# Moving the residual layernorm of a sandwich block from a stage of its own into the attention loop

## The reference

```
a  = layernorm(x)
s  = a @ W_spin.T + b_spin
g  = mean(s, tokens) @ W_global.T
e  = s @ W_J.T
P  = softmax(e @ s.T / 32)
attn = tanh(beta * (s + g + P @ s))
x1 = x + layernorm(attn)
y  = layernorm(x1)
h  = silu(y @ Wg.T / 127) * (y @ Wu.T / 127)     # int weights, 3072 x 1024
out = x1 + layernorm(h @ Wd.T / 127)
```

## Time and profile before

| | before |
|---|---|
| median of 3 runs | 1401.44 us (1400.98 to 1401.98) |
| profiled execution, its own time | 1401.98 us |
| its span on the slowest core (core 0) | 1399.8 us |
| spans of the 8 cores | 1385.7 to 1399.8 us |
| TensorE matmul busy | 1182.5 us, 84% |
| VectorE, ScalarE, GpSimd busy | 372.0, 208.5, 73.1 us |
| idle time of TensorE ahead of L955 | 115.5 us, behind DMA transposes into `xn2T` |
| DMA | 131.00 MB, mean 94 GB/s |

### The profile page before, as it was taken

How to read it: one execution, slowest core, us unless ns; L and a number is a source line. 1 busy time by engine, 2 the same in 40 slices (tenths; PEclk the granted TensorE clock), 3 DMA queues, 4 the chain that set the end, 5 groups by cost and what they waited for, 6 DMA issues and landing times.

```text
span 1399.8 us, 14416 instructions; the slowest of 8 cores (1385.7 to 1399.8 us)
## 1 busy us (share of the span) xinstructions
PE 1182.5 (84%) x5274; PEld 513.5 (37%) x5274; DVE 372.0 (27%) x608; ACT 208.5 (15%) x331; POOL 73.1 (5%) x92
## 2 busy tenths in 40 slices
PE   0788887869999999999999011499999999999997
PEld 0233332223444444444444000144444444444443
DVE  2243343301121111112111545521111122133443
ACT  0111111211122112212221100111111111100000
POOL 0011110000000000000000100111111111000000
PEclk9999998989999999999999555699999999999999
DMA  9746565661223224322321988573645453023322
GB/s 196 151 112 146 140 146 126 157 116 36 45 59 70 53 45 64 71 48 46 68 61 30 222 209 238 130 79 35 86 45 77 46 67 39 1 91 98 113 91 90
DMA packets 230388, 131.00 MB, mean 94 GB/s; under 512 B 204720, under 2 KB 204720, under 8 KB 230320
## 3 DMA queue, kind: packets, MB, share of 16 engines
q1 hardware_dynamic: 102688, 79.74, 22.2%
q0 software_dynamic: 57744, 29.37, 16.1%
q10 hardware_dynamic: 69888, 20.98, 7.3%
HBM read 92.31 MB, written 25.17 MB: 84 GB/s over the span
## 4 chain that ended last, share of the span: by engine, by line
PE 77%; DMA 12%; DVE 6%; issue 2%; SPq 1%; ACT 1%; ACTq 1%; DVEq 0%
PE ps_q L544 16%; PE ps_pv L651 16%; PE ps_d L1103 12%; PE ps_g L955 12%; PE ps_u L967 11%; DMA xnT_sb<-xn_bf 7%; PE ps_s L257 6%; PE ps_e L306 2%; DMA xn2T<-xn_bf 2%; DMA xs<-x 2%; DVE x_buf L822 1%; PE ps_pv L428 1%; PE ps_s L253 1%; SPq L891 1%; DVE ln_tmp L812 1%
## 5 line engine op out<-in xcount | busy, mean ns | idle before, releaser
L955 PE MATMUL ps_g<-xn2T,wg_sb 128*128 128x512 bf16 x768 | 187.8, 389 | 115.5 <-DMA xn2T<-xn_bf 115.5
L544 PE MATMUL ps_q<-s_FM,ebuf 128*128 128x512 bf16 x1024 | 225.6, 381 | 9.1 <-DMA ebuf<-e_sc 9.1
L651 PE MATMUL ps_pv<-s_tok,PT_sb 128*128 128x512 bf16 x1024 | 225.3, 381 | 0.9 <-DVE g_bc L494 0.9
L967 PE MATMUL ps_u<-xn2T,wu_sb 128*128 128x512 bf16 x768 | 183.8, 383 | 0.0
L1103 PE MATMUL ps_d<-wdT_sb,h_act 128*128 128x512 bf16 x768 | 165.9, 379 | 1.1 <-DVE h_act L990 1.1
L955 PEld LDWEIGHTS ps_g<-xn2T,wg_sb 128*128 128x128 bf16 x768 | 76.1, 100 | 210.9 <-issue 124.0
L544 PEld LDWEIGHTS ps_q<-s_FM,ebuf 128*128 128x128 bf16 x1024 | 100.2, 98 | 131.9 <-issue 12.8
L651 PEld LDWEIGHTS ps_pv<-s_tok,PT_sb 128*128 128x128 bf16 x1024 | 100.6, 98 | 123.1 <-issue 3.5
L257 PE MATMUL ps_s<-wspT_sb,xnT_sb 128*128 128x512 bf16 x512 | 136.8, 415 | 0.0
L990 DVE SCALAR_TENSOR_TENSOR h_act<-silu_b,ps_u 128x512 bf16<-128x512 f32 x96 | 65.8, 687 | 262.0 <-PE ps_u L967 262.0
L967 PEld LDWEIGHTS ps_u<-xn2T,wu_sb 128*128 128x128 bf16 x768 | 75.9, 99 | 93.3 <-issue 4.8
(11 more groups left out here) (67 smaller groups left out, 421.0 us busy)
## 6 DMA issues: line engine op xcount, KB each, us to landing
xs<-x SPq DMA_DIRECT2D x24, 1024.0 KB, 7.2
x_sc<-x_buf SPq DMA_DIRECT2D x16, 512.0 KB, 4.6
xs<-x_sc SPq DMA_DIRECT2D x16, 512.0 KB, 4.2
out<-out_b SPq DMA_DIRECT2D x16, 512.0 KB, 5.0
wg_sb<-wgT POOLq DMA_DIRECT2D x24, 256.0 KB, 4.5
wu_sb<-wuT POOLq DMA_DIRECT2D x24, 256.0 KB, 5.6
wdT_sb<-wdT POOLq DMA_DIRECT2D x4, 1536.0 KB, 15.6
e_sc<-e_stage POOLq DMA_DIRECT2D x32, 128.0 KB, 2.5
```

Of the source, the lines that this page charges most:

```text
L544: i = t.matmul(ps_q[:, slot, half * 512:(half + 1) * 512], ebuf[:, qt % 2, j, :], s_FM[:, j, qi * 1024 + half * 512: qi * 1024 + (half + 1 ...
L651: i = t.matmul(ps_pv2[:, nb * 512:(nb + 1) * 512], PT_sb[:, par, cb * P:(cb + 1) * P], s_tok[:, cb, nb * 512:(nb + 1) * 512], start=(cb == ...
L955: i = t.matmul(ps_g[:, slot, :], wg_sb[:, par, j, :], xn2T[:, j, tb * 512:(tb + 1) * 512], start=(j == 0), stop=(j == KC - 1))
L967: i = t.matmul(ps_u[:, slot, :], wu_sb[:, par, j, :], xn2T[:, j, tb * 512:(tb + 1) * 512], start=(j == 0), stop=(j == KC - 1))
```

## The change

The residual stage is split. Its first half (normalise attn, add x, mean and variance of x1, store x1) now stands inside the attention loop, one tile behind (`emit_l2c`); its second half (normalise x1, transpose) stays after the loop, for which each x1 tile is read back from DRAM. The store of attn to DRAM and the loads of it are gone. To make room in SBUF, `P_sb` holds two quarters instead of four, and exp of a quarter waits for the transpose of the quarter two before it. The square root of attn's variance, one instruction over all tiles before, is now one instruction for each tile, in ScalarE's order between tanh and the next exp; the square root of x1's variance is one instruction over all 16 tiles after the loop, where it was one for each four tiles. x is loaded one tile at a time on SyncE's queue, two tiles ahead. In the second half the loads and transposes alternate on SyncE's queue: load, transpose, load, transpose. GpSimd's weight loads now also wait for the last store of x1.

```diff
-        P_sb = eC(nc.sbuf_tensor("P_sb", [P, N], BF16))
+        P_sb = eC(nc.sbuf_tensor("P_sb", [P, 2, 1024], BF16, side="right"))
...
+        def emit_l2c(t):
+            par = t % 2
+            def fsq2(s, t=t, wv=rec[("bn2", t)]):
+                s.wait_ge(sv.h, wv)
+                s.activation(out=sq2c[:, t:t + 1], in_=mv2_all[:, t, 1:2],
+                             func=AF.Sqrt, bias=eps_col[:]).then_inc(ss.h, 1)
+            s_add(fsq2)
...
+            def fch(v, t=t, par=par):
+                v.wait_ge(ss.h, rec[("sq2", t)])
+                i = v.reciprocal(out=rs2c[:, t:t + 1], in_=sq2c[:, t:t + 1])
...
+                i = v.tensor_scalar(out=lnt2[:], in0=attn_wb[:, par, :],
...
+                i = v.tensor_tensor(out=x1c[:, par, :], in0=lnt2[:],
+                                    in1=xs2c[:, par, :], op=ALU.add)
...
+                v.bn_stats(out=st6b[:, 0:6], in_=x1c[:, par, 0:512])
+                i = v.bn_stats(out=st6b[:, 6:12], in_=x1c[:, par, 512:1024])
...
+                i = v.bn_aggr(out=mvb3_all[:, t, :], in_=st6b[:])
...
+            def fx1s(sy, t=t, par=par, sem=sem, wv=rec[("x1v", t)], w_self=sem.n):
+                sy.wait_ge(sv.h, wv)
+                sy.wait_ge(sem.h, w_self)
+                sy.dma_start(out=x1_d.rearrange("(q p) d -> q p d", p=P)[t],
+                             in_=x1c[:, par, :]).then_inc(sem.h, 16)
...
+            if t + 2 < NT_OWN:
+                emit_xld(t + 2, rec[("x1v", t)])
...
-                     wtr=rec.get(("ptr", qt - 1, qi), 0),
+                     wtr=(rec.get(("ptr", qt, qi - 2), 0) if qi >= 2
+                          else rec.get(("ptr", qt - 1, qi + 2), 0)),
...
-            def fdma(s, qt=qt, par=par, wss=rec[("tanh", qt)]):
-                s.dma_start(out=attn_d..., in_=attn_wb[:, par, :])
+            if qt >= 1:
+                emit_l2c(qt - 1)
+            if qt == NT_OWN - 1:
+                emit_l2c(qt)
...
+        for t_i in range(NT_OWN):
+            def fld(sy, ...):          # waits: x1 stored; t_i <= 1: all of attention
+                sy.dma_start(out=x1r[:, par, :], in_=x1_rr[t_i])
+            def fap(v, t_i=t_i, par=par):   # waits: x1r loaded, transpose t_i - 2
+                i = v.tensor_scalar(out=xn2_bf[:, par, :], in0=x1r[:, par, :],
+                                    scalar1=mvb3_all[:, t_i, 0:1],
+                                    scalar2=rsig3[:, t_i:t_i + 1],
+                                    op0=ALU.subtract, op1=ALU.mult)
+            def ftr(sy, ...):
+                sy.dma_start_transpose(out=xn2T[:, :, t_i * P:(t_i + 1) * P],
+                                       in_=xn2_bf[:, par, :])
...
+                    gp.wait_ge(dtm[0].h, pc_done["dt0"])
+                    gp.wait_ge(dtm[1].h, pc_done["dt1"])
```

More of the change, by code:

```diff
@@ L526, in build_program, with emit_xld, f @@
         e_load(1)
+        def emit_xld(t, wv_war):
+            sem = dsm[t % 2]
+            def f(sy, t=t, sem=sem, wv=wv_war, w_self=sem.n):
+                if wv:
+                    sy.wait_ge(sv.h, wv)
+                sy.wait_ge(sem.h, w_self)
+                sy.dma_start(out=xs2c[:, t % 2, :],
+                             in_=x_d.rearrange("(q p) d -> q p d", p=P)[t]
+                             ).then_inc(sem.h, 16)
+            block.sync(f)
+            sem.n += 16
+            rec[("xld", t)] = (sem, sem.n)
@@ L567, in fexp @@
                     s.wait_ge(sv.h, wrs)
-                s.activation(out=P_sb[:, qi * 1024:(qi + 1) * 1024],
+                s.activation(out=P_sb[:, qi % 2, :],
                              in_=ps_q[:, slot, :], func=AF.Exp,
@@ L590, in fptr @@
                     .rearrange("p (j q) -> p j q", j=8),
-                    in_=P_sb[:, qi * 1024:(qi + 1) * 1024]
+                    in_=P_sb[:, qi % 2, :]
                     ).then_inc(sem.h, 16)
@@ L749, in build_program, with l3_s0 @@
[L749 to L755, removed]
+        sqv3 = e2(nc.sbuf_tensor("sqv3", [P, NT_OWN], F32))
+        rsig3 = e2(nc.sbuf_tensor("rsig3", [P, NT_OWN], F32))
+        def l3_s0(s):
@@ L756, in l2_s0 @@
             s.wait_ge(sv.h, pc_done["sv"])
-            i = s.activation(out=sq2_all[:], in_=mv2_all[:, :, 1], func=AF.Sqrt,
-                             bias=eps_col[:])
+            i = s.activation(out=sqv3[:], in_=mvb3_all[:, :, 1], func=AF.Sqrt,
+                             scale=c_sc127[:], bias=c_b127[:])
             vinc(ss, i)
[L760 to L765, removed]
-            vinc(sv, i)
@@ L801, in build_program, with l3_v0 @@
[L801 to L808, removed]
+        block.scalar(l3_s0)
+        ss_sq3 = ss.n
+        def l3_v0(v):
+            v.wait_ge(ss.h, ss_sq3)
+            i = v.reciprocal(out=rsig3[:], in_=sqv3[:])
+            vinc(sv, i)
+        block.vector(l3_v0)
+        sv_l3 = sv.n
+        x1_rr = x1_d.rearrange("(q p) d -> q p d", p=P)
@@ new lines, in build_program, with fld @@
+        for t_i in range(NT_OWN):
+            par = t_i % 2
+            sem = da[par]
+            def fld(sy, t_i=t_i, par=par, sem=sem, w_self=sem.n,
+                    wa=rec.get(("xn2a", t_i - 2), 0)):
+                w = rec[("x1_dma", t_i)]
+                sy.wait_ge(w[0].h, w[1])
+                if t_i <= 1:
+                    sy.wait_ge(st.h, pc_done["st"])
+                    sy.wait_ge(sv.h, pc_done["sv"])
+                    sy.wait_ge(ss.h, pc_done["ss"])
+                    for s_, v_ in pc_done["tr"]:
+                        sy.wait_ge(s_.h, v_)
+                    sy.wait_ge(deL[0].h, deL[0].n)
+                    sy.wait_ge(deL[1].h, deL[1].n)
+                    sy.wait_ge(dsm[0].h, dsm[0].n)
+                    sy.wait_ge(dsm[1].h, dsm[1].n)
+                    sy.wait_ge(dtm[0].h, pc_done["dt0"])
+                    sy.wait_ge(dtm[1].h, pc_done["dt1"])
+                if wa:
+                    sy.wait_ge(sv.h, wa)
+                sy.wait_ge(sem.h, w_self)
+                sy.dma_start(out=x1r[:, par, :], in_=x1_rr[t_i]
+                             ).then_inc(sem.h, 16)
+            block.sync(fld)
+            sem.n += 16
+            rec[("x1rl", t_i)] = (sem, sem.n)
+            def fap(v, t_i=t_i, par=par):
+                w = rec[("x1rl", t_i)]
@@ L899, in build_program, with ftr @@
-        for t_i in range(4):
-            l2_grpA(t_i)
-        l2_sqrt(0)
-        l2_grpB(0)
+            block.vector(fap)
+            rec[("xn2a", t_i)] = sv.n
+            sem_tr = dtp[par]
+            def ftr(sy, t_i=t_i, par=par, sem=sem_tr, wv=sv.n,
+                    w_self=sem_tr.n):
+                sy.wait_ge(sv.h, wv)
+                sy.wait_ge(sem.h, w_self)
+                sy.dma_start_transpose(
+                    out=xn2T[:, :, t_i * P:(t_i + 1) * P],
+                    in_=xn2_bf[:, par, :]).then_inc(sem.h, 16)
@@ L904, in build_program @@
+            block.sync(ftr)
+            sem_tr.n += 16
+            rec[("xtr", t_i)] = (sem_tr, sem_tr.n)
+            if t_i % 4 == 3:
+                rec[("xtr4", t_i // 4)] = (dtp[0].n, dtp[1].n)
         wgT_r = wgT_d.rearrange("(j p) h -> p j h", p=P)
@@ L998, in ffn_group @@
             sb_rd[sbs] = sv.n
-        for g in range(1, 4):
-            for t_i in range(4 * g, 4 * g + 4):
-                l2_grpA(t_i)
-            l2_sqrt(g)
-            l2_grpB(g)
         s_flush()
-        l2_done = dict(sv=rec[("xn2", NT_OWN - 1)],
-                       ss=rec[("sq3g", NT_OWN // 4 - 1)],
+        l2_done = dict(sv=rec[("xn2a", NT_OWN - 1)],
+                       ss=ss_sq3,
                        dt0=dtm[0].n, dt1=dtm[1].n,
```

179 lines of the change are left out of this document (53 added, 126 removed).

## The result

The changed kernel is slower: its runs, compared with those of the kernel before on the same chips, give a ratio of 1.005 (95% interval 1.0028 to 1.0072), about 7 us (between 4 and 10 by the interval); the runs that are compared lie between 1405 and 1418 us, those of before between 1401 and 1404. I had put it at 1396 us, 5 us faster. The median over all its runs, 1411.1 us, holds some in which the cores of one die ran at a lower clock and is not used.

What follows compares the result with a forecast made beforehand. TensorE was taken to bound attention, and a chain of loads, VectorE and DMA transposes the residual stage. -7.4 (stage), +1.4 (loop) and +0.3 (start) gave -5.7 us, from 1401.98 to 1396.3, taken as 1396; 8-in-10 range 1387 to 1412.

Steps and rivals of the forecast that it cites:

- waits in the loop without the last tile: Attention loop: TensorE waiting for the transpose of quarter 1, 0.1 us in each of 14 tiles, +1.4 us, bounds 0 and +16.8.
- period of a tile: Second half after the loop: load, normalise and issue of the transpose, one tile after the other, 6.17 us each.
- collision with the weight loads: Start of the second half: six weight loads share the DMA engines, costing 7.9 us, at least 1.6 and at most 22.5.
- part 1: First half of the stage, moved into the attention loop: transpose of quarter 1 just in time, 0.3 us to spare; +1.4 us.
- part 3: After the loop: 16 tiles of load, normalise, transpose in series, ending at 892.7 against 900.15, -7.4 us.
- The line between 256 and 1024 KB: Load of x1 after the loop: 2.7 us for 256 KB and 5.1 for 1024 give 3.5 for 512; 3.65 taken.
- Part 2: Between loop and second half: tile 15's new chain delays the first load of x1 from 773.6 to 784.3, 10.7 us lost.
- The serial queue gives back the gain: Rival, stage after the loop: at 4.2 us a load the 16 tiles take 8.8 longer; total 1400 to 1404; chance 0.22.
- the transpose of quarter 1 comes late: Rival, attention loop: it lands behind store and load on SyncE's queue, 16.8 us instead of 1.4, total 1411; chance 0.18.
- The signs of being wrong: TensorE waiting in attention for more than 5 us, or the stage ending more than 5 us from the predicted 892.7.
- the order of the semaphore writes: DMA: a transfer's semaphore write lands only after its engine's earlier writes, putting a transpose about 1.0 us behind the load.
- A table change: Rival, ScalarE in the loop: a drain of 1.38 us on top of 1.28, total about 1410; chance 0.05.

Runs made afterwards that it cites:

- e1_last: Changed kernel with the store of x1 and load of x issued behind the transposes of quarters 1 to 3, for tile 13 alone; ratio 1.0009 to the kernel before.
- e6_half: Changed kernel with loads of half a tile of x1 (256 KB instead of 512 KB) after the loop from tile 2 on; ratio 0.9947 to the kernel before.
- e5_nox: Changed kernel without 14 of the 16 loads of x in the attention loop, store of x1 still ahead of the transposes; one execution, 1399.78 us.

## Why the prediction was wrong, step by step

Terms as the prediction put them, against core 0 of the changed kernel:

| term | predicted us | measured us |
|---|---|---|
| transpose of quarter 1, in flight | 5.6 | 5.1 in the last tile, 4.5 to 6.3 from the third on (cores 0, 1) |
| waits in the loop without the last tile | +1.4 | +1.2 |
| last tile of the loop | 0 | +4.4 |
| last matmul of P @ s to first load of x1 | 17.0 | 19.3 |
| load of a tile of x1 | 3.65 | 4.1 |
| period of a tile | 6.17 | 6.65 |
| collision with the weight loads | +7.9 | about +4.5 |
| stage, last matmul to last landing | 125.4 | 131.5 |

Against the 5.7 us of gain stand three misses: a wait in the last tile of the loop that the prediction put at nothing (4.4 us), the size of a period in the stage (7.2 us over 15 of them, less 3.4 by which the collision was overpriced) and the later start of that stage (2.3).

- **The step that failed in part 1 is the deadline.** The length of the delay was right; what it was held against was not the same in every tile. I took 13.81 us of scores between tiles for all of them and multiplied by 14. The last pass has no next tile whose quarter 0 it could compute (`if qt + 1 < NT_OWN`), so 48 matmuls stand there, 10.36 us from their start to that of P @ s, and the second quarter of P @ s wants its transpose 3.45 us earlier. With a margin of 0.3 us elsewhere it had to be about 3 us late; the idle time was 2.60. The code and the trace of before both showed it. e1_last shows the cause: with two issues of one tile moved, the tile takes 13.98 us again. The last tile in the chain of waits of before:

```profile
743.17 10.36 PE ps_q L544 x48
753.53 13.83 PE ps_pv L651 x64
```

- **The wait cost more than itself.** 2.60 us of waiting came to 4.4, since the 48 matmuls behind it took 12.21 us, where the 48 of the scores just before took 10.52. The granted clock in that stretch, core 0 after and then before:

```profile
761.00:773.00 12.00, 11.55 (x46) 4.67 (x44) 0.59 (x3) 0.50 (x2) 0.00 (x0) 0.87 0.12 22
```

```profile
754.00:767.00 13.00, 13.00 (x62) 5.85 (x60) 0.32 (x2) 0.89 (x2) 0.00 (x0) 1.00 0.11 21
```

- **In part 3 the mechanism was right and a size was off.** The tiles run one after another as laid out; but a period is 6.65, not 6.17, and 15 times 0.48 are 7.2 us. 0.4 of the 0.48 is the load, 4.1 instead of 3.65. The line between 256 and 1024 KB mixed tensors of other layouts; the row of the very same shape, 512 KB in 4.2, stood beside it, and the prediction itself names 4.2 as the point at which the gain is gone. The half load of e6_half shows what was off in the line: not its fixed part, but 1.0 to 1.1 us for 256 KB where it had 0.8.
- **Part 2** was 2.3 us short on core 0, since the last store there took 4.55 us against the earlier trace rows; on the other cores of die 0 it is 17.6 to 18.1 after the last matmul, 0.6 to 1.1 short.
- **The collision with the weights** was put too high by some 3 us: the first two periods are 7.4 and 10.4 instead of 6.65, and a transpose was held 1.7 us, not 6.2.
- **The rivals.** "The serial queue gives back the gain" happened; "the transpose of quarter 1 comes late" happened too, with 4.4 us in one tile and 1.2 in five others, where I had priced it at equal amounts in 14. I gave each a chance as if they excluded one another and priced each alone. Together they give what core 0 shows: the loop ends 5.2 us later, the stage is 1.3 shorter, 3.9 in all. The early waits go with loads of x that took 5.3 to 5.8 us on core 0, above the 5.0 that I had taken; later ones took 4.6 to 4.8 and nothing waited until the last tile. Why the early loads were slower stays open.
- **The signs of being wrong** that I had named: the second showed, the stage ends 11.4 us from where I put it (904.1 against 892.7); the first did not, TensorE's idle time behind transposes in attention is 2.9 us on core 0, though the loop lost 5.7.
- **A right number with a wrong reading.** I put the 1.0 us behind the load down to the order of the semaphore writes. In the earlier trace rows too it is the data: though the transpose was issued at 222.86, no packet under 512 B moves from 223.5 to 226.5 us.
- **A table change:** the rule of a drain at a table change (the Trainium skill, ScalarE: Activation LUTs, What ACT_TABLE_LOAD costs) did not show: behind a tanh of 1024 columns the load starts 0.02 us after its end (746.87 + 1.15, then 748.04) and takes 1.28.
- **Right:** ScalarE's, VectorE's and the halved buffer's costs (nothing), the landing of a transpose 0.9 to 1.0 us behind the load ahead of it.

## What to carry to other kernels

A delay is compared with a deadline, and the first and last passes of a pipelined loop have other deadlines than those between; look for the `if` that leaves the next pass's work out. Work taken off a serial chain gains nothing if its place in the queue makes the chain serial again: here over four tenths of the stage's traffic and 48 us of VectorE's work were removed for 1.3 us, and issuing the loads two tiles ahead, with not one byte fewer, gave some 42. Issue what somebody waits for ahead of stores and prefetches that nobody waits for, also where the queue looks idle.

## What the runs showed of the hardware

- After 2.60 us of waiting in an otherwise unbroken run of matmuls the granted clock was 0.87 over the next 12 us instead of 1.00, and that cost 1.7 us. In shorter stretches of that time it was near the lower of its two levels (0.5, or 1.2 GHz) at first and at the upper one (2.4 GHz) from 765 us at the latest:

```profile
760.40:763.00 2.60, 2.60 (x8) 0.96 (x9) 0.32 (x2) 1.10 (x2) 0.00 (x0) 0.57 0.11 21
765.00:767.00 2.00, 2.00 (x11) 0.88 (x10) 0.00 (x0) 0.00 (x0) 0.00 (x0) 1.00 0.00 0
```

- After the 0.65 us of e5_nox it stayed at 1.00:

```profile
759.00:769.00 10.00, 9.79 (x45) 4.53 (x47) 0.32 (x2) 1.21 (x2) 0.00 (x0) 1.00 0.22 41
```

- With two loads in flight instead of one, each load was slower (medians of 4.7 to 5.2 us for 512 KB, instead of 3.75 to 4.1), and the stage still took 88 to 92 us instead of 130 to 134 on cores 0 to 3.
- A DMA transpose of 256 KB landed 3.0 us after its issue alone, 3.6 behind a store of 512 KB and 5.1 behind a store and a load of 512 KB each; its data moved last.
